# Dot-product graph attention in a four-layer kernel: units handled in pairs, turned probabilities copied by one engine per unit

## The reference

```python
# layer 0, one head
scores = einsum('bnd,bmd->bnm', h @ W_q, h @ W_k) * 64**-0.5
scores = where(adj == 0, -1e9, scores)
x = x + softmax(scores) @ (h @ W_v)
# layer 1, four heads with biases
scores = leaky_relu(einsum('bhno,bhmo->bhnm', q, k) / 8, 0.2) + mask
feats  = einsum('bhnm,bhmo->bhno', softmax(scores), v)
x = x + leaky_relu(mean(feats, axis=1), 0.2)
```

## Time and profile before

| | us |
|---|---|
| median of 3 runs | 3477.9 (3467.1 to 3480.51) |
| the profiled execution | 3465.94, span 3464.1 |
| busy in the span: PE / DVE / ACT / POOL | 88% / 87% / 84% / 29% |
| layer 0's units | about 33 to 253 |
| layer 1's units | about 303 to 1229 |
| layers 2 and 3 | from about 1250 to the end |

### The profile page before, as it was taken

How to read it: one execution, slowest core, us unless ns; L and a number is a source line. 1 busy time by engine, 2 the same in 40 slices (tenths; PEclk the granted TensorE clock), 3 DMA queues, 4 the chain that set the end, 5 groups by cost and what they waited for, 6 DMA issues and landing times. The chain is left out here.

```text
span 3464.1 us, 78782 instructions
## 1 busy us (share of the span) xinstructions
PE 3048.9 (88%) x30972; PEld 1673.3 (48%) x30972; DVE 3028.9 (87%) x4698; ACT 2894.3 (84%) x3774; POOL 992.1 (29%) x869
## 2 busy tenths in 40 slices
PE   7987998999999969899899898998998988877875
PEld 5764666666666633333333333333333333336764
DVE  7886887878888779999999999999999999975676
ACT  4555787778788759999999999999999999985675
POOL 5434666666666700000000000000000000005684
PEclk9998999999999989999999999999999999997798
DMA  7640000000000000000000000000000000002121
GB/s 245 221 144 21 22 22 23 20 19 22 21 20 21 20 8 11 11 11 13 8 14 11 10 11 11 10 11 10 11 10 11 11 11 11 11 4 67 51 70 34
DMA packets 68411, 111.58 MB, mean 32 GB/s; under 512 B 26452, under 2 KB 26582, under 8 KB 68054
## 3 DMA queue, kind: packets, MB, share of 16 engines
q1 hardware_dynamic: 68054, 106.69, 10.0%
HBM read 86.61 MB, written 18.87 MB: 30 GB/s over the span
## 5 line engine op out<-in xcount | busy, mean ns | idle before, releaser
L1119 ACT ACTIVATE l_scalar_ring<-l_w,l_r 128x1024 f32<-128x1024 f32 x1568 | 1652.7, 1159 | 34.6 <-DVE l_values L1170 27.6
L1235 DVE TENSOR_SCALAR l_vector_ring<-l_w_code,l_r_code 128x2048 f32<-128x2048 f32 x1264 | 1602.7, 1341 | 2.7 <-PE scores L1044 0.5
L1034 PE MATMUL scores<-l_scalar_ring,l_signs 128*32 128x512 f32 x6272 | 754.6, 599 | 69.4 <-ACT l_scalar_ring L1119 69.0
L1044 PE MATMUL scores<-l_vector_ring,l_signs_code 128*32 128x512 f16 x10112 | 683.4, 392 | 110.3 <-DVE l_vector_ring L1235 107.7
L462 POOL TENSOR_TENSOR l_masked<-l_relu,mask 128x512 f32<-128x512 f32 x512 | 585.5, 1165 | 343.3 <-ACT l_relu L664 321.9
L250 ACT COPY probs_t<-turned 128x512 f32<-128x512 f32 x576 | 324.5, 588 | 395.9 <-PE turned L209 395.9
L172 POOL TENSOR_TENSOR stat<-stat,minus_half 128x8 f32<-128x8 f32 x32 | 71.6, 2237 | 1876.4 <-DVE stat L167 1876.3
L1044 PEld LDWEIGHTS scores<-l_vector_ring,l_signs_code 128*32 128x32 bf16 x10112 | 249.0, 95 | 575.6 <-DVE l_vector_ring L1235 245.8
L277 ACT ACTIVATE l_probs<-l_logits,negmax 128x1024 f32<-128x1024 f32 x384 | 442.8, 1153 | 6.8 <-DVE negmax L268 6.8
L209 PE MATMUL turned<-ident,l_probs 128*128 128x128 f32 x3072 | 435.6, 287 | 11.7 <-issue 7.5
L1034 PEld LDWEIGHTS scores<-l_scalar_ring,l_signs 128*32 128x32 f32 x6272 | 187.8, 109 | 417.5 <-issue 246.4
(11 more groups left out here) (249 smaller groups left out, 2831.2 us busy)
## 6 DMA issues: line engine op xcount, KB each, us to landing
mask<-masks_kept SPq DMA_DIRECT2D x192, 256.0 KB, 2.6
l_adj<-adj SPq DMA_DIRECT2D x64, 512.0 KB, 5.9
masks_kept<-l_mask_ring SPq DMA_DIRECT2D x64, 256.0 KB, 4.8
x_res<-x SPq DMA_DIRECT2D x8, 256.0 KB, 4.9
out<-x_res SPq DMA_DIRECT2D x8, 256.0 KB, 2.9
l_h<-l_h SPq DMA_DIRECT2D x8, 128.0 KB, 2.7
l_kl<-l_dh SPq DMA_DIRECT2D x32, 2.0 KB, 1.8
l_kl<-l_dl SPq DMA_DIRECT2D x32, 2.0 KB, 1.8
```

The source lines that it names most:

```text
L1034: last = nc.tensor.matmul(s.scores[g * ROWS:(g + 1) * ROWS, buf, half, :], signs[:, window], scalar_ring[:, at % SCALAR_RING, g, halves[ha ...
L1044: last = nc.tensor.matmul(s.scores[g * ROWS:(g + 1) * ROWS, buf, half, :], signs_code[:, par, g % 2, window], parts(vector_ring[:, at % VE ...
L1119: last = nc.scalar.activation(scalar_ring[:, at % SCALAR_RING, g, :], w[:, par, :], ACT.Relu, bias=r[:, par, column:column + 1])
L1235: last = nc.vector.tensor_scalar(vector_ring[:, at % VECTOR_RING, g:g + 2, :], w_code[:, par, :, :], r_code[:, par, 0, column:column + 1], ...
```

## The change

Two units with neighbouring numbers (heads 0 and 1, 2 and 3 in layer 1; two row blocks in layer 0) form a pair p = n // 2. ScalarE now copies both halves of `turned` for even units and VectorE both halves for odd units, into four SBUF buffers `probs_t`. TensorE sums a pair in two steps, one in each unit of the pair behind it: the even unit's output into the upper 64 rows of `outT`, the odd one's into the lower 64. `turn_pair` turns both by one matrix product with a block-diagonal `wv_pairs`, one pair later again. VectorE's `copy_out` comes once per pair, at the start of an even unit; both `finish` calls of the pair stand in that same unit, behind `logit` and the inverse row sum. The low part of a fill is taken one unit later in layer 1. `rinv` has 8 slots. The first two graphs are written out ahead of the hardware loop, which has two turns now, and the last two pairs stand behind the last graph.

```diff
-def copy_half(eng, copy, s, sems, half, u):
+def copy_half(eng, copy, s, sems, half, u, to=None):
...
+    PAIRED = max(1, H // 2)
+    Q = U // 2
...
+        wv_pairs = sb("wv_pairs", [P, PAIRED, P], F32)
+        probs_t = sb("probs_t", [P, 4, NB, P], F32)
+        rinv = sb("rinv", [P, 8], F32)
...
-            def graph(b, par, project, last_graph):
+            def turn_pair(q, p):
+
+                pe.wait_ge(sems["out_copied"], STARTS + q + 1)
+                wait(pe, sems["unit_done"], STARTS + 2 * q)
+                nc.tensor.matmul(pair_out, s.turned_out[:], wv_pairs[:, p % PAIRED, :], start=True, stop=True
+                                 ).then_inc(sems["out_turned"], 1)
+
+            def pair_times_values(par, q, p, step):
+
+                if step == 0:
+                    pe.wait_ge(sems["half0_copied"], STARTS + 2 * q + 2)
+                    pe.wait_ge(sems["half1_copied"], STARTS + 2 * q + 2)
+                    wait(pe, sems["out_copied"], STARTS + q)
+                    wait(pe, sems["unit_done"], STARTS + 2 * q)
+                for j in range(step * NB // 2, (step + 1) * NB // 2):
+                    for odd in range(2):
+                        last = nc.tensor.matmul(s.outT[odd * D:(odd + 1) * D, 0:P], values[:, par, j, :],
+                                                probs_t[:, p % 2 * 2 + odd, j, :], start=(j == 0), stop=(j == NB - 1),
+                                                skip_group_check=True)
...
+            def graph(b, par, project, last_graph, first=False):
                 for n in range(U):
                     u = b * U + n
+                    p = n // 2
                     turn_probs(pe, s, sems, probs[:, n % 2, :], u)
-                    if n > 0:
-                        turn_out(pe, s, sems, u - 1, 0, unit_out, weights=wv[:, (n - 1) % H, :])
+                    if n % 2 == 0 and not (first and p < 2):
+                        turn_pair(b * Q + p - 2, (p - 2) % Q)
...
-                    wait(pe, sems["unit_done"], STARTS + u)
-                    if n == 0:
+                    if n == 2:
                         pe.wait_ge(sems["values_ready"], b + 1)
-                    probs_times_values(pe, s, sems, values[:, par, :, :], u)
-                turn_out(pe, s, sems, b * U + U - 1, 0, unit_out, weights=wv[:, H - 1, :])
+                    if not (first and p < 1):
+                        pair_times_values(par if p else 1 - par, b * Q + p - 1, (p - 1) % Q, n % 2)
...
-                    copy_half(a, nc.scalar.copy, s, sems, 1, u)
+                    if n % 2 == 0:
+                        for half in range(2):
+                            copy_half(a, nc.scalar.copy, s, sems, half, u, probs_t[:, n % 4, :, :])
...
+            def finish_pair(b, p):
+
+                v.drain()
+                finish(b, 2 * p, b * U + 2 * p)
+                if leaky:
+                    v.drain()
+                finish(b, 2 * p + 1, b * U + 2 * p + 1)
...
-                    v.drain()
-                    copy_half(v, nc.vector.tensor_copy, s, sems, 0, u)
-                    if n > 0:
-                        finish(b, n - 1, u - 1)
+                    p = n // 2
+                    if n % 2 == 0 and not (first and p < 2):
+                        copy_out(v, s, sems, b * Q + p - 2)
+                    if n % 2:
+                        for half in range(2):
+                            copy_half(v, nc.vector.tensor_copy, s, sems, half, u, probs_t[:, n % 4, :, :])
                     if not last_graph or n + 2 < U:
                         logit(b, (n + 2) % U, u + 2)
-                    inverse_sum(n)
+                    inverse_sum(n, u)
+                    if n % 2 == 0 and not (first and p < 2):
+                        if p < 2:
+                            finish_pair(b - 1, p - 2 + Q)
+                        else:
+                            finish_pair(b, p - 2)
...
-                    copy_out(v, s, sems, u)
-                    for k in fills_at(n, project):
+                    for k in fills_at(n - 1 if leaky else n, project):
                         take_fill(b + 1, 1 - par, k)
```

More of the change, by code:

```diff
@@ L243, in turn_out @@
                        start=True, stop=True).then_inc(sems["out_turned"], 1)
-def copy_half(eng, copy, s, sems, half, u):
+def copy_half(eng, copy, s, sems, half, u, to=None):
     eng.wait_ge(sems["turned_ready"], STARTS + u + 1)
     n = s.NB // 2
-    copy(s.probs_t[:, half * n:(half + 1) * n, :], s.turned[:, half * n:(half + 1) * n, :]
+    copy((s.probs_t if to is None else to)[:, half * n:(half + 1) * n, :], s.turned[:, half * n:(half + 1) * n, :]
          ).then_inc(sems[f"half{half}_copied"], 1)
@@ L372, in fills_at @@
         def fills_at(n, project):
-            if not project:
+            if not project or n < 0:
                 return []
@@ L589, in score @@
                     nc.tensor.matmul(out, h1[:, par, rows], kl[:, par, h, cols], start=False, stop=True).then_inc(sems["scores_ready"], 1)
-            def graph(b, par, project, last_graph):
+            def turn_pair(q, p):
[14 more added lines that the diff above has]
+                                                skip_group_check=True)
+                if step == 1:
+                    last.then_inc(sems["out_ready"], 1)
+            def graph(b, par, project, last_graph, first=False):
                 for n in range(U):
                     u = b * U + n
+                    p = n // 2
                     turn_probs(pe, s, sems, probs[:, n % 2, :], u)
-                    if n > 0:
-                        turn_out(pe, s, sems, u - 1, 0, unit_out, weights=wv[:, (n - 1) % H, :])
+                    if n % 2 == 0 and not (first and p < 2):
+                        turn_pair(b * Q + p - 2, (p - 2) % Q)
                     if n + 3 < U:
@@ L636, in _ @@
                 score(0, 0, u, u)
-            with pe.Fori(0, B // 2 - 1) as t:
-                for par in range(2):
-                    graph(2 * t + par, par, True, False)
+            graph(0, 0, True, False, first=True)
+            graph(1, 1, True, False)
+            with pe.Fori(0, (B - 4) // 2) as t:
+                for i in (2, 3):
+                    graph(2 * t + i, i % 2, True, False)
             graph(B - 2, 0, True, False)
             graph(B - 1, 1, False, True)
+            turn_pair(B * Q - 2, Q - 2)
+            for step in range(2):
+                pair_times_values(1, B * Q - 1, Q - 1, step)
+            turn_pair(B * Q - 1, Q - 1)
         @block.scalar
@@ L749, in scale_half, with inverse_sum @@
                     variance(v, s, s.stat, s.stat[:, 2, :]).then_inc(sems["seed_ready"], 1)
-            def inverse_sum(n):
-                slot = n % 4
-                nc.vector.reciprocal(s.rinv[:, slot:slot + 1], s.rowsum[:, slot:slot + 1])
+            def inverse_sum(n, u):
+                v.wait_ge(sems["probs_ready"], u + 1)
+                nc.vector.reciprocal(rinv[:, n % 8:n % 8 + 1], s.rowsum[:, n % 4:n % 4 + 1])
             def finish(b, n, u):
                 i, h = n // H, n % H
-                slot = n % 4
-                v.wait_ge(sems["out_turned"], u + 1)
+                scale = rinv[:, n % 8:n % 8 + 1]
+                v.wait_ge(sems["out_turned"], b * Q + n // 2 + 1)
                 xb = s.block(b, i)
+                unit_out = pair_out[:, n % 2 * D:(n % 2 + 1) * D]
                 if not leaky:
-                    nc.vector.scalar_tensor_tensor(out=xb, in0=unit_out[:, 0:D], scalar=s.rinv[:, slot:slot + 1], in1=xb,
+                    nc.vector.scalar_tensor_tensor(out=xb, in0=unit_out[:, 0:D], scalar=scale, in1=xb,
                                                    op0=ALU.mult, op1=ALU.add).then_inc(sems["unit_done"], 1)
@@ L766, in finish @@
                 if h == 0:
[L767 removed]
+                    nc.vector.scalar_tensor_tensor(out=acc[:], in0=unit_out[:, 0:D], scalar=scale,
                                                    in1=v_bias[:], op0=ALU.mult, op1=ALU.add).then_inc(sems["unit_done"], 1)
                 else:
[L770 removed]
+                    nc.vector.scalar_tensor_tensor(out=acc[:], in0=unit_out[:, 0:D], scalar=scale,
                                                    in1=acc[:], op0=ALU.mult, op1=ALU.add).then_inc(sems["unit_done"], 1)
@@ L800, in graph @@
                         take_values(b + 1, 1 - par)
-                v.drain()
-                finish(b, U - 1, b * U + U - 1)
             nc.vector.memset(one[:], 1.0)
@@ L818, in _ @@
             nc.vector.tensor_scalar(up[:], s.ident[:], UP, None, ALU.mult)
+            nc.vector.memset(wv_pairs[:], 0.0)
+            v.drain()
             v.wait_ge(sems["weights_in"], 16 * WEIGHT_LOADS)
+            for odd in range(2):
+                rows = slice(odd * D, (odd + 1) * D)
+                nc.vector.tensor_copy(wv_pairs[rows, :, rows], wv[rows, min(odd, H - 1):H:2, :])
             hold_waits(v, sems)
@@ L884, in _ @@
```

(11 more changed lines are left out.)

4 lines of the change are left out of this document (2 added, 2 removed).

## The result

The changed kernel takes 3586.0 us (median of 4 runs, 3577.2 to 3592.5), the kernel before 3479.2 in the same runs: ratio **1.031, 95% interval 1.028 to 1.035**. The forecast was 3563 with a range of 3500 to 3625, and slower.

The account below looks back on a forecast made before the run. No engine was full before; after the change a loop of waits through GpSimd's masked scores and both finishes was to bound layer 1. 3465.9 + 78 + 12 + 1 = 3557, plus 6 for the median: 3563 us, range 3500 to 3625.

Parts of the forecast that it names:

- The ring: Layer 1 wait loop: odd transposes, scores, rectified and masked scores, even logits, both finishes, products, next odd transposes; 7.84 us a pair.
- The same with and without fills: Layer 1: a pair closes at 7.84 us with or without a fill, since everything else has cover.
- Layer 1, 78 more: Layer 1: 128 x 7.84 plus 4 for a jump makes 1007.5 us, 78 more than the 930 before.
- The one jump left: Layer 1's hardware loop: the remaining jump costs 4 us (3.76 idle and a spell at half clock); the 930 before hold two.
- VectorE waits 0.8 for the mask: Layer 1, even units: VectorE is ready for the logits at O + 3.84 and waits 0.81 us for GpSimd's masked scores.
- The two candidates for the ring: Layer 1: loop through GpSimd's masked scores, 7.84 us a pair (chance 0.72), or VectorE's own work, 7.03 (chance 0.09).
- Layer 0, 12 more: Layer 0: VectorE's own work closes the loop at 6.84 us a pair, 29.65 a graph; 236 us against 223.
- Bounds of the copies: VectorE: by the drain rule copies start 0.69 apart, not 0.61, finishes 0.28, not 0.19; layer 0 about 8 us more.
- VectorE's chain alone: Layer 1: masked scores come early, VectorE's own work closes the loop at 7.03 us a pair; total 3459; chance 0.09.
- ScalarE's and TensorE's chain: Layer 1: even unit ScalarE 3.57, odd TensorE 2.89, fill 0.43; 6.78 a pair; layer 0 about 6 less; 3408; chance 0.08.
- The clock rival: Layer 1: TensorE, less busy, gets a granted clock of 0.93; 55 us more, total 3618; chance 0.11.
- the 6 added for the median: Total: the profiled execution lies 12 us below the median shown; half of the gap, 6, is added to every case.

Follow-up runs that it names:

- the short mask step: Changed kernel with GpSimd adding the mask to only 256 of the 512 columns of each half in layer 1: 3474.0 us, ratio 1.001.
- the finishes first: Changed kernel with VectorE finishing the pair ahead of the even unit's logits and inverse row sum, not behind them: 3443.6 us, ratio 0.993.
- the kernel before's finish late: Kernel before with VectorE finishing unit u-1 behind the logits and inverse row sum of unit u, not ahead of them: 3822.3 us, ratio 1.101.
- the copies shared: Changed kernel with ScalarE copying the second half and VectorE the first half of every unit: 3866.5 us, ratio 1.115.

## Why the prediction was right, and where it was off

- **The ring.** Right in every link and in its place. Predicted 7.84, measured 7.96: transposes to scores 0.93 (0.90), scores to rectified scores 0.64 (0.63), on to GpSimd 0.67 (0.66), to the logits 2.46, to the first finish 1.52 (1.46), then 0.72 (0.71) and 1.02. The piece behind the inverse row sum, which the trace of before did not show, was the worst known and the largest miss, 0.06.
- **The same with and without fills.** Right: the metronome alternates 5.6 and 2.4, nearly all pairs take 7.87 to 8.10, and most of those of the last graph, which has no fills, 8.0 to 8.1.
- **Layer 1, 78 more.** It was 90.9, 13 more than forecast: 0.12 a pair is 15 of it, and the first two pairs, which have no finish to wait for, give 3 back (6.8 and 6.3 us). The one jump left fits its term: TensorE is idle 2.7 us there and the pair around it takes 10.3, 2.4 more than its neighbours. Whether one jump fewer saved anything is not shown: writing the graphs out changed nothing in a run of its own, but its interval of 6 us either way would hide 4.
- **VectorE waits 0.8 for the mask.** Right: 91.3 us over the 116 waits of both lines, 0.79 each. Its own chain is a little longer than the 7.03 worked out, as the short mask step shows (7.07 in the median pair). The two candidates for the ring lay 0.8 us apart by the prediction's sum and 0.9 as measured, well above the errors of their links.
- **Layer 0, 12 more.** It was 18.0 between its units and 2.7 at the way to layer 1. The sum for a graph was too small: pairs with fills take 7.55 to 8.3 instead of 7.6 to 7.7, the one without any 6.9, where 6.84 was forecast. Most of it is the first pair of a graph, 8.2 to 8.3 where the sum has 7.57. That pair took 8.15 in the kernel before as well; what sets it was not followed up.
- **Bounds of the copies.** Two copies in a row took 1.27 to 1.29 us, so 0.6 between their starts, as the prediction had from the row. That is less than the 0.69 by the rule which the prediction quotes from the Trainium skill ("VectorE: DVE Perf Modes", The DRAIN you can't avoid); the same section adds that an operation which isn't held starts earlier, which the prediction left out and with which these copies agree.
- **The rivals.** VectorE's chain alone gives 3474 with the short mask step, where 3459 was priced; it needed a shorter GpSimd step to become true. ScalarE's and TensorE's chain was priced at 3408; with the finishes first the kernel reaches 3444. In layer 1 it takes 6.94 a pair instead of 6.78, where the output copy still holds the pair's turn for 41.4 us, and layer 0 with its end is 6 us longer than before, not 6 shorter. No row shows that case's 0.43 for a fill or its 6 us for layer 0. The clock rival did not happen: 0.99 at 82% busy.
- **23 us short in the total.** The profiled executions differ by 122.6 where 91 were forecast. Of these 32, 13 are in layer 1, 8 in layer 0 with its end, and 11 behind layer 1, where nothing changed; against that stand the 6 added for the median and the 2.5 by which the profiled execution lay above its own median. That the 11 behind layer 1 and these 8.5 nearly cancel is luck; what was forecast well is the ring.

## What to carry to other kernels

When a step is moved behind another in one engine's queue, ask what waits for the moved step, and what the step now ahead of it waits for: here a 0.28 us finish inherited the wait for a mask that had stood on no path to the products before, and closed a ring over all four engines. Follow such a ring once around with durations from the trace and divide by the units it covers; by busy times alone this change would have looked like a small gain. And a part that costs nothing or gains nothing inside a ring (the late low parts, the copies by one engine) has to be judged again once the ring is open.

## What the runs showed of the hardware

TensorE's clock did not follow its mean busy share. With the kernel before's finish late, TensorE was busy 869 of 1199 us (72%) and its clock 0.99; with the copies shared it was busy 974 of 1290 (76%, partly because of the slower clock) and the clock 0.86. What differs in the rows besides is the idle time: in the first, gaps of about 1.4 us in most units of 4.5; in the second, gaps of mostly 1.9 to 3.0 us once in a pair of 10; in the changed kernel, with a clock of 0.99 too, gaps of 0.8 to 1.8 once in 8. The Trainium skill ("TensorE: Matmul & The Clock Gate", Part 1) says that the gate goes by how busy the array has been recently. In these three layers the lower clock goes with the longer gaps, and a mean over a layer doesn't tell when; that the gaps are the cause is not shown, as no run varied only their length. Nor is the clock the same in each execution of the same code: layer 3's units had 0.83 to 0.87 in nine profiles and 0.91 to 0.92 in three, and took 10 to 18 us less in those.
